# Softmax sums of an attention loop: one row per head, inverted and spread by matmuls, with the product one pair later

## What is computed

```python
scores = jnp.einsum('bqhd,bkhd->bhqk', q, k) * SCALE          # attention 0 adds rotary angles and a causal mask
attn = jax.nn.softmax(scores, axis=-1)
out = jnp.einsum('bhqk,bkhd->bqhd', attn, v).reshape(B, S, D)
h = h + out @ Wo.T + bo                                        # attention 1: quantised projections instead
```

## Time and profile before

| | |
|---|---|
| runs | 356.75, 357.86, 362.52 us |
| the profiled execution, its own time | 357.03 us |
| its span, from the first to the last instruction | 355.2 us |
| mean granted TensorE clock | 0.966 of full speed |
| TensorE matmul busy | 328.6 us (93%) |
| VectorE busy | 194.9 us (55%) |
| ScalarE busy | 131.7 us (37%) |
| GpSimd busy | 79.5 us (22%) |

### The profile page before, as it was taken

The page is one execution under the profiler, slowest core; times in us unless marked ns, Lnnn a source line. Parts: engine busy times, 40 slices in busy tenths (PEclk is TensorE's granted clock), DMA queues, the critical chain, the costliest instruction groups (busy, mean ns, idle before and its releaser), DMA issues.

```text
span 355.2 us, 8094 instructions
## 1 busy us (share of the span) xinstructions
PE 328.6 (93%) x3086; PEld 282.5 (80%) x3086; DVE 194.9 (55%) x563; ACT 131.7 (37%) x302; POOL 79.5 (22%) x118
## 2 busy tenths in 40 slices
PE   8999997999897999997788998879999999999995
PEld 6876775777696999895566777557999999998994
DVE  6978669887641333317765787776622242232335
ACT  2443754772533334431453674044111122111220
POOL 1323377500232000014225410100500000000041
PEclk9999999999998999999899999856999999999999
DMA  7950118997946822353960002950347897339813
GB/s 261 280 164 0 68 45 294 352 426 292 422 180 233 337 93 58 127 205 102 397 286 2 2 0 59 421 233 0 98 160 301 340 359 294 149 81 347 344 45 113
DMA packets 20740, 70.76 MB, mean 199 GB/s; under 512 B 4386, under 2 KB 13172, under 8 KB 15716
## 3 DMA queue, kind: packets, MB, share of 16 engines
q1 hardware_dynamic: 19028, 65.75, 50.0%
q0 software_dynamic: 1680, 4.59, 3.7%
HBM read 61.56 MB, written 7.56 MB: 195 GB/s over the span
## 4 chain that ended last, share of the span: by engine, by line
PE 60%; DVE 20%; DMA 8%; issue 4%; ACT 4%; POOL 2%; DVEq 1%; SPq 0%; POOLq 0%
PE psum L1216 19%; PE psum L1225 14%; PE psum L638 4%; PE psum L509 4%; DVE srec L835 3%; DMA arena<-w 3%; DVE smax L825 2%; DVE sc L829 2%; PE psum L632 2%; PE psum L976 2%; PE psum L578 2%; DMA xw<-slots_in 1%; PE psum L1195 1%; DMA arena<-xp 1%; POOL slots_in L1105 1%
## 5 line engine op out<-in xcount | busy, mean ns | idle before, releaser
L1216 PEld LDWEIGHTS psum<-xwT,arena 128*128 128x128 f32 x736 | 84.3, 192 | 1.3 <-issue 0.7
L1216 PE MATMUL psum<-xwT,arena 128*128 128x128 f32 x736 | 84.7, 275 | 0.3 <-DMA arena<-w 0.3
L1225 PE MATMUL psum<-arena,prob 128*128 128x256 f32 x272 | 63.2, 387 | 0.0
L1225 PEld LDWEIGHTS psum<-arena,prob 128*128 128x128 f32 x272 | 51.5, 194 | 6.6
L1365 ACT ACTIVATE act_a<-psum 128x128 f32<-128x128 f32 x72 | 20.0, 278 | 80.6 <-PE psum L1216 79.9
L1287 DVE TENSOR_TENSOR prob<-psum,act_a 128x128 f32<-128x128 f32 x72 | 21.0, 292 | 42.8 <-ACT act_a L1365 42.8
L1358 ACT ACTIVATE prob<-psum,par_s 128x128 f32<-128x128 f32 x64 | 23.5, 368 | 38.7 <-PE psum L1216 34.2
L578 PE MATMUL psum<-causal_b,identb 128*128 128x296 bf16 x185 | 33.8, 324 | 2.3 <-DMA xd_z<-slots_out,slot_gi 1.4
L1110 POOL DMA_DIRECT2D slots_out<-zw x15 | 8.4, 557 | 122.7 <-DVE zw L1298 78.5
L578 PEld LDWEIGHTS psum<-causal_b,identb 128*128 128x128 bf16 x185 | 18.8, 111 | 11.2 <-DMA xd_z<-slots_out,slot_gi 1.8
L874 POOL TENSOR_TENSOR arena<-arena,cst 128x296 f32<-128x296 f32 x32 | 21.7, 698 | 0.0
(11 more groups left out here) (233 smaller groups left out, 515.5 us busy)
## 6 DMA issues: line engine op xcount, KB each, us to landing
arena<-w SPq DMA_DIRECT2D x28, 1024.0 KB, 10.3
arena<-w SPq DMA_DIRECT2D x10, 2048.0 KB, 8.2
arena<-xp SPq DMA_DIRECT2D x5, 384.0 KB, 6.0
slots_out<-zw POOLq DMA_DIRECT2D x15, 128.0 KB, 6.1
xw<-slots_in SPq DMA_DIRECT2D x15, 128.0 KB, 3.8
slots_in<-zero SPq DMA_DIRECT2D x1, 1792.0 KB, 7.0
slots_out<-zero SPq DMA_DIRECT2D x1, 1792.0 KB, 12.9
arena<-arena SPq DMA_DIRECT2D x16, 74.0 KB, 1.9
```

Source lines behind the costliest of these rows:

```text
L1216: last = nc.tensor.matmul(bank(1 + f % 4)[:, part * WIN:(part + 1) * WIN], w1v[:, k, part * FF + f * P:part * FF + (f + 1) * P], rows[:, k ...
L1225: last = nc.tensor.matmul(bank(into)[:, 0:D], hid[:, f, :], w2v[:, f, :], start=(f == 0), stop=(f == FC - 1))
```

## The change

The sums of the exponentials go to one row per head. A new table `head_sum` (46 columns, a band of ones) is cut so that the eight sum matmuls add up into one place: rows 0 to 15, 74 columns, of the pair's output bank. VectorE inverts these 16 rows of 74 columns (`sums_vector`). TensorE then spreads the 16 reciprocals to the 128 output rows by two matmuls (`spread_sums_tensor`) with the new table `head_rows`, into the columns of the bank where the sums were before. ScalarE copies the raw outputs from PSUM to `oT` (`raw_scalar`), since VectorE then multiplies the spread reciprocals in PSUM with `oT` in place, one pair later than before (`output_vector` of p - 3 in step p). Each step on TensorE has one filler in both attentions. The first two steps of the loop (pairs 2 and 3) are written out ahead of it. `mask_values_scalar` is not changed: it waits for the same count of products. The tables grow from 80 to about 98 KB (`const_rows`) and by 46 columns of 128 rows (`const`).

```diff
@@ tables
+        "head_sum": (np.arange(46)[None, :] == 14 + p // SEQ),
...
+    row, chunk = np.arange(P)[None, :], np.arange(DC)[:, None]
+    head_of_row = (8 * (row // 64) + 4 * chunk + 2 * ((row // 32) % 2) + (row // HD) % 2).reshape(-1)
...
+        "head_rows": (head_of_row[None, :] == np.arange(IMAGES)[:, None]),
...
-        srec = sb("srec", [P, DC * PW])
+        srec = sb("srec", [HEADS, 2, PW])
@@ scores_tensor
-                keep_warm(pe, 2 * buf, 2 + 2 * layer)
+                keep_warm(pe, 2 * buf, 1)
@@ output_tensor
-                    last = nc.tensor.matmul(dst[row:row + 32, (DC + c) * PW:(DC + c + 1) * PW], table("head2", PW)[:, 0:2 * HD],
+                for g in range(8):
+                    last = nc.tensor.matmul(dst[0:32, 2 * DC * PW:(2 * DC + 1) * PW], table("head_sum", PW)[:, 14 - 2 * g:46 - 2 * g],
                                             pT[:, buf, g, :].rearrange("p (j q) -> p j q", j=2)[:, :, 0:SEQ],
-                                            start=True, stop=True, tile_position=(0, row))
+                                            start=(g == 0), stop=(g == 7), tile_position=(0, 0))
                 last.then_inc(s("o_ps"), 1)
+
+            def raw_taken(pe, p):
+
+                pe.wait_ge(s("raw"), done + p + 1)
+
+            def spread_sums_tensor(pe, p, buf):
+
+                for c in range(DC):
+                    last = nc.tensor.matmul(bank(6 + buf)[:, (DC + c) * PW:(DC + c + 1) * PW], head_rows[:, c * P:(c + 1) * P],
+                                            srec[:, buf, :], start=True, stop=True)
+                last.then_inc(s("rec_ps"), 1)
@@ tensor
-                with pe.Fori(1, PAIRS // 2) as u:
+                for p in (2, 3):
+                    scores_tensor(pe, p, p % 2)
+                    turn_probs_tensor(pe, p - 1, 1 - p % 2)
+                    if p == 3:
+                        raw_taken(pe, 0)
+                    output_tensor(pe, p - 2, p % 2)
+                    if p == 3:
+                        spread_sums_tensor(pe, 0, 0)
+                with pe.Fori(2, PAIRS // 2) as u:
                     for b in range(2):
                         p = u * 2 + b
                         scores_tensor(pe, p, b)
                         turn_probs_tensor(pe, p - 1, 1 - b)
+                        raw_taken(pe, p - 3)
                         output_tensor(pe, p - 2, b)
+                        spread_sums_tensor(pe, p - 3, 1 - b)
...
                 turn_probs_tensor(pe, PAIRS - 1, 1)
+                raw_taken(pe, PAIRS - 3)
+                spread_sums_tensor(pe, PAIRS - 3, 1)
                 output_tensor(pe, PAIRS - 2, 0)
                 output_tensor(pe, PAIRS - 1, 1)
+                raw_taken(pe, PAIRS - 2)
+                spread_sums_tensor(pe, PAIRS - 2, 0)
+                raw_taken(pe, PAIRS - 1)
+                spread_sums_tensor(pe, PAIRS - 1, 1)
                 finish(1)
@@ output_vector
+            def sums_vector(dve, p, buf):
+                dve.wait_ge(s("o_ps"), done + p + 1)
+                nc.vector.reciprocal(srec[:, buf, :], bank(6 + buf, HEADS)[:, 2 * DC * PW:(2 * DC + 1) * PW]).then_inc(s("srec"), 1)
+
             def output_vector(dve, p, buf):
-                dve.wait_ge(s("o_ps"), done + p + 1)
-                nc.vector.reciprocal(srec[:], bank(6 + buf)[:, DC * PW:2 * DC * PW]).then_inc(s("srec"), 1)
-                dve.wait_ge(s("srec"), done + p + 1)
+                dve.wait_ge(s("raw"), done + p + 1)
+                dve.wait_ge(s("rec_ps"), done + p + 1)
...
-                    nc.vector.tensor_tensor(dst, raw, rec, ALU.mult).then_inc(s("o_read"), 1)
+                    nc.vector.tensor_tensor(dst, rec, dst, ALU.mult).then_inc(s("o_read"), 1)
...
-                dve.wait_ge(s("o_read"), read + p + 1)
@@ vector
                     for b in range(2):
                         p = u * 2 + b
                         softmax_vector(dve, p, b)
-                        output_vector(dve, p - 2, b)
+                        sums_vector(dve, p - 2, b)
+                        output_vector(dve, p - 3, 1 - b)
+                output_vector(dve, PAIRS - 3, 1)
+                sums_vector(dve, PAIRS - 2, 0)
+                sums_vector(dve, PAIRS - 1, 1)
                 output_vector(dve, PAIRS - 2, 0)
                 output_vector(dve, PAIRS - 1, 1)
@@ scalar
+            def raw_scalar(act, p, buf):
+
+                act.wait_ge(s("srec"), done + p + 1)
+                nc.scalar.activation(oT[:, :, bass.ds(p * PW, PW)], bank(6 + buf)[:, 0:DC * PW].rearrange("p (c n) -> p c n", c=DC),
+                                     ACT.Copy).then_inc(s("raw"), 1)
...
+                    if not early(p):
+                        raw_scalar(act, p - 2, buf)
                     if not (isinstance(p, int) and p == 0):
                         mask_values_scalar(act, p - 1, 1 - buf)
...
                     act.wait_ge(s("pT_ps"), done + p + 1)
-                    if not early(p):
-                        act.wait_ge(s("o_ps"), done + p - 1)
...
+                raw_scalar(act, PAIRS - 2, 0)
+                raw_scalar(act, PAIRS - 1, 1)
```

More of the change, by code:

```diff
@@ L130, in vit_tower @@
         cst_rows = sb("cst_rows", CONST_ROWS.shape)
-        image_of, patch_row = cst_rows[:, 0:ROWS], cst_rows[0:2, ROWS:2 * ROWS]
+        image_of, head_rows, patch_row = cst_rows[:, 0:ROWS], cst_rows[:, ROWS:ROWS + DC * P], cst_rows[0:2, ROWS + DC * P:]
         ident = table("ident")
@@ L831, in softmax_vector @@
                                         ALU.subtract).then_inc(s("sc_read"), 1)
+            def sums_vector(dve, p, buf):
+                dve.wait_ge(s("o_ps"), done + p + 1)
+                nc.vector.reciprocal(srec[:, buf, :], bank(6 + buf, HEADS)[:, 2 * DC * PW:(2 * DC + 1) * PW]).then_inc(s("srec"), 1)
             def output_vector(dve, p, buf):
-                dve.wait_ge(s("o_ps"), done + p + 1)
-                nc.vector.reciprocal(srec[:], bank(6 + buf)[:, DC * PW:2 * DC * PW]).then_inc(s("srec"), 1)
-                dve.wait_ge(s("srec"), done + p + 1)
+                dve.wait_ge(s("raw"), done + p + 1)
+                dve.wait_ge(s("rec_ps"), done + p + 1)
                 dst = oT[:, :, bass.ds(p * PW, PW)]
-                raw = bank(6 + buf)[:, 0:DC * PW].rearrange("p (c n) -> p c n", n=PW)
-                rec = srec[:].rearrange("p (c n) -> p c n", n=PW)
+                rec = bank(6 + buf)[:, DC * PW:2 * DC * PW].rearrange("p (c n) -> p c n", c=DC)
                 if layer == 0:
-                    nc.vector.tensor_tensor(dst, raw, rec, ALU.mult).then_inc(s("o_read"), 1)
+                    nc.vector.tensor_tensor(dst, rec, dst, ALU.mult).then_inc(s("o_read"), 1)
                 else:
-                    nc.vector.scalar_tensor_tensor(out=dst, in0=raw, scalar=wmean[:, 2:3], in1=rec, op0=ALU.mult,
+                    nc.vector.scalar_tensor_tensor(out=dst, in0=rec, scalar=wmean[:, 2:3], in1=dst, op0=ALU.mult,
                                                    op1=ALU.mult).then_inc(s("o_read"), 1)
-                dve.wait_ge(s("o_read"), read + p + 1)
             def vector(dve, do):
@@ L854, in vector @@
                     softmax_vector(dve, p, p)
-                    nc.vector.memset(srec[:, 0:1], 0.0).then_inc(s("o_read"), 1)
+                    dve.sem_inc(s("o_read"), 1)
                 if layer == 0:
@@ L858, in vector @@
                 dve.wait_ge(s("o_read"), read)
-                with dve.Fori(1, PAIRS // 2) as u:
+                for p in (2, 3):
+                    softmax_vector(dve, p, p % 2)
+                    sums_vector(dve, p - 2, p % 2)
+                output_vector(dve, 0, 0)
+                with dve.Fori(2, PAIRS // 2) as u:
                     for b in range(2):
```

## The result

The changed kernel takes 374.53 us, median of 4 runs (373.05 to 377.34), against 358.31 for the kernel before beside it: a ratio of 1.0425, 95% interval 1.0371 to 1.0479. It is slower, inside the predicted range and 4 us above the predicted time. The profiled execution took 375.68 us (span 373.7). Some runs of these kernels come out longer at a lower clock, so ratios compare the faster runs alone and are not the quotients of the medians given.

What follows compares the result with a forecast made beforehand. TensorE and VectorE were both taken as full in the loop over pairs. Loops 4.0 and 3.25 plus the stretches behind them 3.9 and 2.35 gave 13.5 on 357.0: 370.5 us, range 361 to 376.

Steps and rivals of the forecast that it cites:

- TensorE and VectorE are both full: Loop over pairs: VectorE savings show only as far as TensorE shortens; work added to TensorE shows at once.
- The 3.65 us on VectorE: Loop of attention 1: one step from reciprocal to next but one, on VectorE alone without waiting for another engine.
- The sums, +0.5: TensorE, each pair: all eight sums in one strip lose their overlap, 1.75 us against 1.21.
- a sign of being wrong: TensorE's outputs in the loop: the prediction would be wrong if sum passes start beside value passes.
- The spread, 0.55: TensorE, each pair: two new matmuls, four passes at 0.12 us plus 0.09 for the change of tile shape.
- Loop of attention 1, +3.25: Six outputs at 0.5 and four spreads at 0.55, less 1.95 for fillers dropped: +3.25 us.
- Loop of attention 0, +4.0: Five outputs at 0.5, four spreads at 0.55, less 0.5 for fillers and 0.2 for short waits: +4.0 us.
- After the loops, +3.9 and +2.35: Behind each loop, serial steps from output 5 through the last spread: +3.9 us in attention 0, +2.35 in attention 1.
- The clock, rival 3: TensorE's clock falls behind or in the loops, lengthening one pair and part of a second: 376 us, chance 0.07.
- Loads exposed, rival 4: Each sum pass is paced by its weight load, 0.7 us more in each of 13 outputs: 379.6 us, chance 0.07.
- VectorE's relief counts, rival 1: New matmuls fit beside others, so VectorE still decides and saves 0.6 on 14 pairs: 348.6 us, chance 0.05.
- The ring has 0.5 to spare: Loop: product and masks take about 2.1 us after the sums; TensorE needs its next values after 2.6.

Runs made afterwards that it cites:

- 4: The kernel before the change with one filler a pair in both attentions and nothing else; 360.74 us, ratio 1.0079.
- the order alone: The kernel before the change with only its output matmul groups reordered over four strips (0, 32, 64, 96 and again); 360.59 us, ratio 1.0023.
- 10 to 12: Kernel before the change: product moved between maximum and subtraction, one filler, four-strip group order, 355.21 us; that order only, 360.59; product and filler, 357.11.
- 1: The changed kernel with its eight sum matmuls spread in turn over four strips of output rows instead of one; 369.44 us, ratio 1.034.
- 2: The changed kernel with each spread issued twice, four matmuls instead of two; 385.64 us, ratio 1.0814.
- 9: The changed kernel with fillers in two waits behind each loop, six ahead of output 7 and three ahead of the last spread; 372.09 us, ratio 1.0306.
- 5: The changed kernel with the masks waiting for the sums of pair p - 2 instead of its product; 370.89 us, ratio 1.0346.
- 6: The changed kernel with projection 1 moved between outputs 6 and 7 and projection 2 ahead of the last two spreads; 372.08 us, ratio 1.0386.
- 8: The changed kernel with each reciprocal preceded by a second one into a tile nobody reads; 381.33 us, ratio 1.0595.
- 3: The changed kernel with the earlier fillers, 2 a pair in attention 0 and 4 in attention 1; 380.98 us, ratio 1.0617.

## Why the prediction was right, point by point

- *TensorE and VectorE are both full; what is added to TensorE shows at once*: right. With TensorE alone made shorter (4, and the order alone in 10 to 12) nothing is won; shortening both gains 0.4 us a pair (10 to 12). The 3.65 us on VectorE was the longer of two kinds of pair, with an idle time of 0.42 behind its product; the one before it is 3.31 (204.14 to 207.45 in the same chain), and the mean is TensorE's 3.48.
- *The sums, +0.5*: the mechanism was right (1), the size was +0.30. Two of the sixteen sum passes start beside the last values (0.13 less; the row at 217.85), which the prediction had named as a sign of being wrong, and the spread starts some 0.1 instead of 0.2 behind the last sum's stream.
- *The spread, 0.55*: 0.59, at 0.11 a pass (2).
- *Loop of attention 1, +3.25*: 2.55. Each of six outputs was charged 0.2 too much; some 0.5 came back, the most of it in spreads of 0.59 and a wait for masks (0.18) that the sum didn't have. *Loop of attention 0, +4.0*: 4.09, but that is luck, since errors cancel: the sums again, against two idle times that the sum didn't have. One is a wait for masks (0.27 at 63.60 us). In the other, in one step of the loop's first turn, TensorE waited in the middle of the values for nothing that the profile shows; its cause stays open:

```profile
72.49 0.42 PE L769 MATMUL psum<-arena 74*32 74x37 f32 x18 [0.34 <-issue]
```

- *After the loops, +3.9 and +2.35*: 3.87, and 4.56 of which 2.3 is the clock (9 leaves 10.20 - 7.95 = 2.25). Order, waits and their releasers came out as told; 5 and 6 confirm them.
- *The clock, rival 3*: not in the sum, and the largest miss, 1.6 us from projection 1 to 4 and 2.3 ahead of the last statistic. The profiled run grew by some 5 us more than the 13.5 of the sum: these 3.9, and 1.9 in stages put at 0, less 0.6 in the loops. What the 1.9 are is not shown; the stage behind the last statistic took 133 to 136 us in other kernels here too. I had the clock fall on whole pairs, at a chance of 0.07; it fell on the ends, behind waits of 0.82, 0.88 and 0.43 us that the sum itself contained. The step that failed is the one that took the row of projections and fillers as following "unchanged": projections 1 and 2 took 3.61 instead of 1.99 us. That the total stayed in the range, the profiled run by 0.3 us and one run of the four (377.34) not, is owed to the upper end, which rival 3 had set.
- *Loads exposed, rival 4*: refuted for the sums. L773 runs 14 passes in 1.06 us, 0.064 from start to start, in one strip, while a load of these lasts 0.11. The rule of the Trainium skill (TensorE: Matmul & The Clock Gate, "Part 3: Packing small matmuls — row/col tiling"), that loads overlap only with another row group, does not describe this; nor does it describe the spread, whose passes go at 0.11 with loads of 0.187.
- *VectorE's relief counts, rival 1*: refuted by 17.7 us of VectorE waiting for sums, and by 8, where 0.62 more on VectorE lengthened a pair by 0.18.
- *The ring has 0.5 to spare*: wrong in size. In attention 1 it has 0.00 to 0.14 (8). The prediction had 2.1 us from the end of the sums to the end of the masks, and TensorE back after 2.6; measured are 2.46 with the signal (219.00 to 221.32, and 0.14) and 2.48 (219.00 to 221.48). That TensorE decides is right by 5, but barely.

## What to carry to other kernels

When two engines are full in a loop, a change has to be priced on both, and work moved from one to the other is worth nothing until the receiver has room; look for work that can fill the waits of the engine that decides (the product between two dependent instructions) before adding work elsewhere. A ring of waits through other engines needs every signal in its sum before it is called slack. Small matmuls on TensorE are priced by how many output strips are in turn, not by their count alone. Behind a loop, write the chain of waits out step by step, and ask of each new wait what the clock does in the stretch behind it.

## What the runs showed of the hardware

- Matmuls into different strips of 32 output rows overlap, and those into one strip follow at 0.064 us for 74 float32 columns; over four strips 12 passes take 0.45 us. They do not start in program order either: all value matmuls stand ahead of all sums in the program, yet in 1 a row of sums (L773) starts at 214.47, ahead of the last value row (L768) at 214.49, and in after at 217.85, ahead of values at 217.87. The Trainium skill (TensorE: Matmul & The Clock Gate, "Part 3: Packing small matmuls — row/col tiling") says that matmuls start and end strictly in program order; these rows show otherwise for the starts in different strips.
- Extra matmuls that nobody reads can save time when they fill a wait (9: ratio 1.0306 instead of 1.0425), and cost their full length when TensorE has none (3: 0.38 us a pair in attention 1).
